# Four chained low-rank layers on one Trainium2 core: the first 128x128 block of W2 loaded from ScalarE's queue and rounded by VectorE

## The reference, cut to what matters

```
x = x + _L0_cond_ref(x, itok_B_0_15, L0_cond_weights)
x = x + _L1_cond_ref(x, itok_B_0_15, L1_cond_W, L1_cond_lora_A, L1_cond_lora_B)
x = x + _L2_cond_ref(x, itok_B_0_2, L2_cond_W, L2_cond_lora_A, L2_cond_lora_B_w)
x = x + _L3_cond_ref(x, itok_B_0_7, L3_cond_W, L3_cond_Wr, L3_cond_A, L3_cond_B)
```

## Time and profile before

| | before |
|---|---|
| median of three runs | 522.36 us (522.11 to 522.70) |
| the profiled execution | 522.34 us |
| its span in the trace | 520.5 us |
| PE busy | 515.3 us (99% of the span) |
| DVE, ACT, POOL busy | 333.8, 201.6, 168.8 us |
| the chain that ended last | PE 96%, DMA 1%, DVE 1%, SP's queue 1% |
| granted clock of PE | 1.00 over the span |
| DMA | 46.80 MB, mean 90 GB/s |

### The profile page before, as it was taken

One profiled execution on the slowest core, in us unless ns is written; L12 is line 12 of the kernel. 1 busy time (PEld: TensorE's weight loads), 2 busy tenths in 40 slices (PEclk: granted clock), 3 DMA queues, 4 the chain that ended last, 5 costly groups with the idle time before them and its releaser, 6 DMA issues.

```text
span 520.5 us, 8870 instructions
## 1 busy us (share of the span) xinstructions
PE 515.3 (99%) x2720; PEld 449.6 (86%) x2720; DVE 333.8 (64%) x655; ACT 201.6 (39%) x351; POOL 168.8 (32%) x250
## 2 busy tenths in 40 slices
PE   8999999999999999999999999999999999999997
PEld 7999999988988888888887788888888888888886
DVE  3798886799433333399877864756647557476464
ACT  4745643355223232367434233323332333233322
POOL 2550000002102020229556434354254434552400
PEclk9999999999999999999999999999999999999999
DMA  8912210214420202040703303213233132222312
GB/s 263 375 62 42 57 40 1 82 40 129 158 107 0 82 0 82 0 167 6 237 3 118 122 21 126 92 48 107 82 116 121 39 112 86 68 88 81 118 35 81
DMA packets 29631, 46.80 MB, mean 90 GB/s; under 512 B 12052, under 2 KB 17940, under 8 KB 29476
## 3 DMA queue, kind: packets, MB, share of 16 engines
q1 hardware_dynamic: 29412, 45.85, 26.8%
q0 software_dynamic: 192, 0.59, 0.3%
HBM read 33.39 MB, written 13.04 MB: 89 GB/s over the span
## 4 chain that ended last, share of the span: by engine, by line
PE 96%; DMA 1%; DVE 1%; SPq 1%; ACT 0%; issue 0%; POOL 0%; ACTq 0%
PE bank L1892 26%; PE bank L1826 15%; PE bank L1758 11%; PE bank L1881 8%; PE bank L1800 6%; PE bank L1812 5%; PE bank L1972 4%; PE bank L1940 4%; PE bank L1948 4%; PE bank L1729 4%; PE bank L1713 3%; PE bank L1943 1%; PE bank L1942 1%; DMA w2raw<-in_w_dram 1%; PE bank L1902 1%; SPq L470 0%
## 5 line engine op out<-in xcount | busy, mean ns | idle before, releaser
L1892 PE MATMUL bank<-t_hi,em_hi 128*128 128x512 f32 x168 | 57.5, 403 | 0.0
L1182 DVE TENSOR_TENSOR w1t_lo<-raw,w1t_hi 128x1024 fp32r<-128x1024 f32 x18 | 24.6, 1369 | 23.3 <-ACT w1t_hi L911 17.1
L686 POOL TENSOR_TENSOR tmp<-raw 128x512 f32<-128x512 f32 x4 | 7.2, 1792 | 97.3 <-DVE raw L1368 97.3
L1892 PEld LDWEIGHTS bank<-t_hi,em_hi 128*128 128x128 f32 x168 | 31.2, 189 | 7.1 <-DVE em_hi L1182 0.4
L1826 PE MATMUL bank<-te,em_hi 128*128 128x512 f32 x144 | 34.9, 395 | 0.0
L1826 PEld LDWEIGHTS bank<-te,em_hi 128*128 128x128 f32 x144 | 27.0, 188 | 6.6
L672 POOL CAST em_hi<-tba 128x256 fp32r x32 | 13.3, 444 | 59.7 <-PE bank L1881 56.0
L1182 DVE TENSOR_TENSOR em_hi<-tmp,em_hi 128x512 fp32r<-128x512 f32 x22 | 15.1, 687 | 21.7 <-ACT em_hi L1018 12.6
L676 POOL TENSOR_TENSOR em_lo<-tba,em_hi 128x256 fp32r<-128x256 f32 x32 | 27.1, 867 | 2.4 <-POOL em_hi L672 1.2
L1758 PE MATMUL bank<-em_hi,w2s_hi 128*128 128x384 f32 x80 | 27.0, 337 | 0.0
L1758 PE MATMUL bank<-em_lo,w2s_hi 128*128 128x384 f32 x80 | 27.0, 337 | 0.0
(11 more groups left out here) (309 smaller groups left out, 1613.0 us busy)
## 6 DMA issues: line engine op xcount, KB each, us to landing
raw<-in_x_dram SPq DMA_DIRECT2D x16, 512.0 KB, 4.0
b1s<-b1scr SPq DMA_DIRECT2D x32, 217.5 KB, 2.7
raw<-in_b1w_dram SPq DMA_DIRECT2D x10, 512.0 KB, 3.2
out_dram<-ef SPq DMA_DIRECT2D x16, 256.0 KB, 2.1
out_dram<-ost SPq DMA_DIRECT2D x15, 256.0 KB, 2.4
graw<-in_w3a3wr_dram SPq DMA_DIRECT2D x4, 768.0 KB, 11.1
b1scr<-b1stage SPq DMA_DIRECT2D x12, 256.0 KB
w2raw<-in_w_dram SPq DMA_DIRECT2D x6, 384.0 KB, 7.0
```

The costliest lines, as they stand in the source:

```text
L1182: V.tensor_tensor(dst, src, f32(hi), ALU.subtract).then_inc(signal, 1)
L1892: ins = nc.tensor.matmul(to[:, :], left[a][:, k0 + k, :], m_right(right, z, k), start=(name in OPENS and n == 0), stop=(n == 3 * KH - 1), ...
```

## The change

Piece 0 of W2 is no longer issued by SP as its second load, but by ACT as its first instruction; every later load of SP stands one place further up. Its hi part is made by a tensor_copy of VectorE, ahead of that engine's first lo part, and not by ACT; it has a semaphore of its own, s_w2d, so all counts of s_w2h are one lower. Of the transposes ahead of the first matmul there are 10 and not 12. Nothing is added to or taken from what is computed.

```
-        WARM = 12
+        WARM = 10
...
-                sp.dma_start(w2raw[k][:, lo_:hi_], w2[k * P:(k + 1) * P, lo_:hi_]).then_inc(s_win[n], 16)
+                if n:
+                    sp.dma_start(w2raw[k][:, lo_:hi_], w2[k * P:(k + 1) * P, lo_:hi_]).then_inc(s_win[n], 16)
...
+            act.dma_start(w2raw[0][:, 0:P], w2[0:P, 0:P]).then_inc(s_win[0], 16)
             act.wait_ge(s_tab, 1)
...
                 if opens_row(n):
                     g_hi(k)
+                if n == 0:
+                    continue
...
             for n, (k, lo_, hi_) in enumerate(W2PIECES):
+                if n == 0:
+                    dve.wait_ge(s_diag, DIAG["w", 0])
+                    V.tensor_copy(W2S[0][:, 0, lo_:hi_], w2raw[0][:, lo_:hi_]).then_inc(s_w2d, 1)
                 if opens_row(n):
                     g_lo(k)
-                dve.wait_ge(s_w2h, n + 1)
+                if n == 0:
+                    dve.wait_ge(s_w2d, 1)
+                else:
+                    dve.wait_ge(s_w2h, n)
...
-                    pe.wait_ge(s_w2l if a else s_w2h, w2_there(k, blocks_[0]))
+                    if a:
+                        pe.wait_ge(s_w2l, w2_there(k, blocks_[0]))
+                    elif w2_there(k, blocks_[0]) == 1:
+                        pe.wait_ge(s_w2d, 1)
+                    else:
+                        pe.wait_ge(s_w2h, w2_there(k, blocks_[0]) - 1)
```

More of the change, by code:

```diff
@@ L295, in cond_resid_kernel @@
         s_w2h = sem("s_w2h")
+        s_w2d = sem("s_w2d")
         s_w2l = sem("s_w2l")
@@ L1217, in _ @@
             for n, (k, lo_, hi_) in enumerate(W2PIECES):
+                if n == 0:
+                    dve.wait_ge(s_diag, DIAG["w", 0])
+                    V.tensor_copy(W2S[0][:, 0, lo_:hi_], w2raw[0][:, lo_:hi_]).then_inc(s_w2d, 1)
                 if opens_row(n):
                     g_lo(k)
-                dve.wait_ge(s_w2h, n + 1)
+                if n == 0:
+                    dve.wait_ge(s_w2d, 1)
+                else:
+                    dve.wait_ge(s_w2h, n)
                 lo(W2S[1][:, k, lo_:hi_], w2raw[k][:, lo_:hi_], W2S[0][:, k, lo_:hi_], s_w2l)
-            dve.wait_ge(s_w2h, W2ALL)
+            dve.wait_ge(s_w2h, W2ALL - 1)
             lo(W2S[1][:, :, FIRST:], w2all[:, :, FIRST:], W2S[0][:, :, FIRST:], s_w2l)
```

## The result

The changed kernel took 523.21 us (median of 15 runs, 522.41 to 523.73), the kernel before, on the same chip, 522.05 (15 runs, 521.41 to 522.70). The ratio is 1.0022, with an interval of 1.0015 to 1.0028; the medians differ by 1.16 us. The forecast was 522.0, within 521.6 to 522.6 and a gain; it came out as a loss, by the mechanism of the third rival. One of the 131 runs of the kernel before that this document rests on took 851 us at a granted clock of 0.56; it is counted nowhere.

The account below looks back on a forecast made before the run. PE was taken to bound the kernel, with row 2's load, POOL and ACT ahead of its unbroken work from 11.95. Only row 2's 0.35 us counted, other terms 0: 522.34 - 0.35 = 521.99, forecast 522.0 us, range 521.6 to 522.6.

Parts of the forecast that it names:

- third rival: TensorE's clock rises later, at 8.4, after PE stands before its first matmul: 0.7 us slower, 523.1; chance 0.05.
- If the rise stays where it is, near 5.66: PE's slow first matmuls: with the clock's rise unmoved, 0.2 us won ahead leave about 0.05, worth 0 at the end.
- the two transposes fewer: Ahead of the first matmul: ten end at 3.95, PE stands 0.32 us until 4.27; worth 0, clock effect aside.
- The rival's own rule: PE at the slow clock: each us does only 0.54 of its work, so each us of later rise costs 0.46.
- PE already stood 0.15 us before the first matmul and rose: Argument against a later clock rise: in the kernel before, PE waited 0.15 us there and its clock still rose.
- The first block: W2's piece 0, issued at 0.79 instead of 1.23: lands 0 to 0.44 us earlier, taken as 0.25.
- SP's places: SP's load queue: row 2's load issued 0.47 us earlier, at 4.07, and landing 0.35 us earlier.
- the hole at 2.80: DMA engines from 2.80 to 3.40: share 0.56, 109 GB/s, 0.39 us idle, which SP's earlier 192 KB piece would fill.
- Row 2 to PE: Row 2 of W2 through POOL and ACT: landing 10.05, PE at 11.60, so the 0.35 us arrive in full.
- the gap of 0.44: PE, free at 11.51, waits 0.44 us for row 2's hi part until 11.95; all this stage can give.
- ACT's issue: ACT issuing the load ahead of the table load: costs some 0.43 us, hidden with 0.6 us to spare.
- DVE's copy: Hi part of W2's first block on DVE: taken as 0.29 us, G's lo part queued behind it.

Follow-up runs that it names:

- e4: The kernel before with only the load of W2's first block moved to ACT's queue, 12 transposes: ratio to before 1.0021, median 522.82 us.
- e11: The changed kernel with 16 transposes instead of 10: ratio to the kernel before 1.0004, median 522.04 us.
- e3: The changed kernel with 14 transposes instead of 10: ratio to the kernel before 1.0005, median 521.74 us.
- e12: The changed kernel with its 10 transposes held back behind ScalarE's dummy exponential: ratio to the kernel before 1.0008, median 522.09 us.
- e1: The changed kernel with 12 transposes instead of 10: ratio to the kernel before 1.0016, median 522.75 us.
- e9: The kernel before with only the first block's hi part made by VectorE, load and 12 transposes as before: ratio 0.9996, median 521.80 us.
- e5: The kernel before with 15 transposes instead of 12: ratio to before 0.9992, median 521.86 us.
- e2: The kernel before with 10 transposes instead of 12: ratio to before 1.0019, median 522.92 us.
- e10: The kernel before with G's row 1 loaded from ACT's queue instead of SP's, and 13 transposes: ratio to before 1.0020, median 522.91 us.
- e7: The kernel before with 10 transposes held back behind ScalarE's dummy exponential: ratio to before 1.0000, median 522.18 us.

## Why the prediction was wrong

**The step that failed** is "If the rise stays where it is, near 5.66", and with it the term for the two transposes fewer ("Worth 0, their effect on the clock aside"). It did not stay. Row 2 was forecast on PE at 11.60 and came at 13.80, since the profiled rise came near 10.3; the runs were 1.16 us slower in the median, where 0.35 were to be gained. The transposes were only one of two ways to it: the load alone, with all twelve, costs as much (e4), because the first block came late and made a pause too. The third rival named this place and mechanism, took 0.7 us for it from a rise at 8.4, and got a chance of 0.05. That its 523.1 lies so near the measured 523.21 is luck: it started from 522.36 and a rise at 8.4, the measurement from 522.05 and, in the profile, a rise at 10.3. The rival's own rule, 0.46 us for each us at the slow level, gives from a rise 4.7 us late 2.1 us, less 0.44 and plus 0.22 for the later first matmul: 1.9, which fits. What spoke against it, "PE already stood 0.15 us before the first matmul and rose", was one execution of a kernel that has 8 runs of 130 over 523 itself.

**The first block**: forecast 0.25 us earlier, measured 0.30 later in the profile of the change (0.31 in e4 and e11, about 0.4 in e3 and e12, 0.87 in e1). I had bounded it from 0 to 0.44 earlier and left out the side below nothing, though I had noted myself that both loads share the engines. This made the pause 0.79 instead of 0.32.

**SP's places**: right in kind, a little small. Row 2 was issued 0.47 us earlier (4.07); the hole at 2.80 was filled (share 1.06). Row 2's hi part begins at 10.73 on average over the six profiles with the loads of before, and at 10.26 over the seven with a row-0 load on ACT's queue: 0.47 us, where I took 0.35. Within either group the profiles differ by 0.38 and 0.66 us, so the 0.99 of this one pair is in good part scatter. The rule of the Trainium skill that I weighed ("DMA: Bandwidth & Descriptors", "Issuing engines are not separate DMA queues"), that only the issuing time is saved, agrees with these 0.47, one place; with this scatter, that the figure is so exact is luck.

**Row 2 to PE**: the gap of 0.44 was as large as said, but in the changed kernel the gain never reached the end: PE itself came later. With the pause filled (e3, e11) PE reaches row 2 at 11.95 and 12.23, after its data. Only the profiles of e4 and e12, with an early rise, have PE at row 2 before 11.95 (11.61 and 11.75).

**ACT's issue** took its time ahead of the table load and was hidden, as said: the table load moved from 0.79 to 1.23, and ACT stood 0.88 us before G's row 0.

**DVE's copy** took 0.23 us (0.29 taken), G's lo part ran behind it, and in e9 the part is worth nothing that shows, as forecast.

**The parts do not add.** Load alone 1.0021, transposes alone 1.0019, together 1.0022. Each makes a pause, of 0.45, 0.58 and 0.79 us in the profiles, and within their intervals the three losses are the same; why the longer pause costs no more is not shown.

## What to carry to other kernels

Work that only keeps TensorE's clock up has to reach the first real matmul without a pause, with a margin for the latest landing of that matmul's data, not for the one in the trace; three transposes too many cost nothing that shows here (e5), two too few 1 us (e2). A load moved to another queue brings forward those behind it by one place, but the one that is waited for first can land later. Where an issue really stands is read from the trace and not from the program: in e10 it came more than a microsecond before the instruction that it was written behind. Where the unknown sits in a single profiled execution, look at the spread of the runs before trusting its value.

## What the runs showed of the hardware that was not expected

- The rise of TensorE's clock is not at one place. In the 14 profiles it lies between 5.6 or before (e4, whose third matmul at 5.60 is fast) and 10.3 us, and one and the same kernel has runs at 521.2 and at 523.9 (e1). The Trainium skill says in "TensorE: Matmul & The Clock Gate", "Part 1: The HAM clock gate (the "warmup" mystery)", that the point varies from run to run, by half a microsecond either way; these runs agree that it varies, and here it does so by more. They add that kernels with a pause of 0.45 to 0.98 us between the transposes and the first matmul have about half of their runs over 523, and those without it one in twenty.
- A load that is issued earlier can land later. The 64 KB block was taken up at 3.53 to 3.61 when it was SP's second load, issued at 1.23 (4.02 in e7, without a cause that I can name), and at 3.90 to 4.47 when ACT's queue issued it at 0.79. In those kernels it was issued together with G's row 0 (196 KB), and the next piece (192 KB) 0.48 us sooner; which of the two delays it is not separated. In e10 it had one more load of 196 KB ahead of it and was taken up at 4.46.
- ACT's queue issued a load at 0.95, while the table load ran (0.79 to 2.07), though the load is written behind the exponential that ran at 2.08 (e10).
- The granted clock reads 1.00 while the matmuls step at the level of 1.2 GHz. The starts of two groups and the number of matmuls between them are the safer reading.
